# A four-layer graph network in fp32: value rows projected in their own group, next weights spread over six units, stores waited for in the next pass, own bias of the last graph pass on VectorE

## What is computed

```python
# L0, and L3 with other weights and its bias added once: attention with 12 heads of 32 in each graph
q, k, v = heads(x @ Wq.T), heads(x @ Wk.T), heads(x @ Wv.T + bv)
scores  = q @ k.T * 384**-0.5 + adj + adj
p       = softmax(where(any(scores != 0), scores, -inf)), nan_to_num
layer   = (p @ v) @ Wo.T + bo
# L1: q, k, v with biases; adj masks and is added with factor beta; no output matrix
# L2: twice (own weights in each):
attn    = softmax(h @ h.T / sqrt(384)) * adj, rows divided by their sum
ctx     = (attn * upper) @ (h @ Wl.T + bl) + diag(attn) * (h @ Ws.T + bs) + (attn * lower) @ (h @ Wr.T + br)
h       = relu((ctx - mean) / std * gain + shift)
```

## Time and profile before

| | |
|---|---|
| median of three runs | 2626.3 us (2626.18 to 2629.85) |
| the profiled execution | 2625.92 us, of which its span 2624.2 us |
| granted TensorE clock, mean | 0.975 |
| busy: PE / DVE / ACT / POOL | 2445.8 (93%) / 1966.2 (75%) / 1605.0 (61%) / 1966.9 (75%) us |
| passes begin (first matmul after the barrier) | l1 638.1, l20 1176.3, l21 1585.1, l3 2015.4 us |

### The profile page before, as it was taken

The page is one execution under the profiler, slowest core; times in us unless marked ns, Lnnn a source line. Parts: engine busy times, 40 slices in busy tenths (PEclk is TensorE's granted clock), DMA queues, the critical chain, the costliest instruction groups (busy, mean ns, idle before and its releaser), DMA issues. The chain is left out here.

```text
span 2624.2 us, 64888 instructions
## 1 busy us (share of the span) xinstructions
PE 2445.8 (93%) x21554; PEld 2097.4 (80%) x21554; DVE 1966.2 (75%) x3543; ACT 1605.0 (61%) x3414; POOL 1966.9 (75%) x2127
## 2 busy tenths in 40 slices
PE   6999999996999999959999998999997999999997
PEld 5888888885877777748888887888886888888886
DVE  4777788785788888877777776776765677777876
ACT  4667666664666556634544554766665666766665
POOL 4888888884677777765566566999996778888886
PEclk9999999997999999969999998999998999999998
DMA  7222232223433333316323316434343222223211
GB/s 138 67 67 70 69 75 69 59 62 70 85 77 79 79 76 79 80 55 114 72 63 73 70 49 127 102 93 104 90 105 83 51 68 68 70 68 73 61 46 52
DMA packets 320602, 200.71 MB, mean 76 GB/s; under 512 B 243426, under 2 KB 320484, under 8 KB 320484
## 3 DMA queue, kind: packets, MB, share of 16 engines
q1 hardware_dynamic: 317028, 197.93, 32.3%
q10 hardware_dynamic: 3456, 1.28, 0.3%
HBM read 136.22 MB, written 62.91 MB: 76 GB/s over the span
## 5 line engine op out<-in xcount | busy, mean ns | idle before, releaser
L491 PE MATMUL l_ps_p<-xT,w 128*128 128x512 f32 x2304 | 593.7, 404 | 59.1 <-PEq L1588 15.1
L491 PEld LDWEIGHTS l_ps_p<-xT,w 128*128 128x128 f32 x2304 | 425.2, 191 | 154.3 <-issue 39.1
L431 POOL TENSOR_TENSOR l_pr<-l_sc,l_st 128x768 f32<-128x768 f32 x192 | 286.4, 1492 | 176.9 <-DVE l_st L826 176.9
L1353 ACT ACTIVATE l_hlr<-l_ps_h 64x384 f32<-64x384 f32 x512 | 248.8, 486 | 250.1 <-PE l_ps_h L1273 241.4
L836 DVE TENSOR_REDUCE l_st<-l_pr 128x12 f32<-128x768 f32 x192 | 182.8, 952 | 244.3 <-ACT l_pr L703 244.3
L385 POOL TENSOR_TENSOR v<-v,l_bvs 128x768 f32<-128x768 f32 x192 | 359.7, 1873 | 0.0
L1199 POOL TENSOR_TENSOR l_hlr<-l_hlr,l_sides 128x768 f32<-128x768 f32 x128 | 235.8, 1842 | 133.1 <-ACT l_hlr L1353 129.5
L1273 PE MATMUL l_ps_h<-second,xT 128*128 128x384 f32 x1728 | 332.2, 342 | 0.0
L1273 PE MATMUL l_ps_h<-w,xT 128*128 128x384 f32 x1728 | 324.7, 342 | 0.0
L1273 PEld LDWEIGHTS l_ps_h<-second,xT 128*128 128x128 f32 x1728 | 300.1, 189 | 29.8 <-issue 28.7
L1273 PEld LDWEIGHTS l_ps_h<-w,xT 128*128 128x128 f32 x1728 | 299.5, 189 | 29.8 <-issue 27.5
(11 more groups left out here) (144 smaller groups left out, 4577.5 us busy)
## 6 DMA issues: line engine op xcount, KB each, us to landing
rows<-l_yo SPq DMA_DIRECT2D x256, 192.0 KB, 1.9
xa<-rows SPq DMA_DIRECT2D x256, 192.0 KB, 4.2
l_xr<-rows SPq DMA_DIRECT2D x192, 192.0 KB, 2.4
l_xr<-in_x SPq DMA_DIRECT2D x64, 192.0 KB, 2.4
out<-l_yo SPq DMA_DIRECT2D x64, 192.0 KB, 1.9
xa<-in_x SPq DMA_DIRECT2D x62, 192.0 KB, 4.2
l_edge<-in_adj SPq DMA_DIRECT2D x80, 128.0 KB, 2.3
raw<-in_L_gnn_Wk SPq DMA_DIRECT2D x12, 144.0 KB, 6.6
```

What stands on the lines that cost most here:

```text
L431: nc.gpsimd.tensor_tensor(pr[b][:, :, :], sc[b][:, :, :], st[b][:, 0, :].unsqueeze(2).to_broadcast([P, HEADS, NODES]), ALU.subtract).then_ ...
L491: last = nc.tensor.matmul(bank[:, :], W[m][:, l, t, o * P:(o + 1) * P], rows[:, r, t, :], start=c + t == 0, stop=c == 2 and t == KT - 1)
L1353: i = nc.scalar.activation(hlr[b][half * NODES:(half + 1) * NODES, g, :], ps_h[m][g * NODES:(g + 1) * NODES, :D], ACT.Copy)
```

## The change

It has six parts.

1. **Value rows.** `AHEAD` now begins with the four v and `exists`, `made` and `bank_of` are rewritten so that v of group i are made in group i and only q and k in group i−1. Before group 0 stand six projections (`AT_FIRST`), and the last group has four. ScalarE waits and TensorE's waits on its copies are rewritten (`act_first`, `act_k2` for the last k tile). Where unit 3 has nothing in gap 0, ScalarE does gap 1 before exp.
2. **Rows' low parts.** GpSimd makes the last tile of group i+1 in unit 0 and two tiles of group i+2 in units 2 and 3, in place of two and one.
3. **Weights of the next pass.** Two steps in each of the last six units (`steps_at`); turned ones go through two SBUF tiles `wt` in place of the projections' banks.
4. **Stores.** The tiles `yo` and their semaphores are shared by all passes; the wait for a pass's stores moves to SP's stream at the next pass's start.
5. **l21's own bias.** The tenth matmul, its bias row's preparation and ScalarE's copy go; VectorE does `itself` and the diagonal as in l20.
6. **GpSimd's tail** in the graph passes adds residual rows one step earlier.

```diff
@@ attention_pass
+        wt = [a.sb(f"wt{b}", [P, D]) for b in range(2)] if nxt and nxt.turned else None
-        yo = [a.sb(f"yo{b}", [P, D]) for b in range(2)]
+        yo, s_out = shared.yo, shared.s_out
+        out_base = 16 * (units // 2) * me.k
...
-        AHEAD = (("q", 0), ("q", 1), ("q", 2), ("k", 0), ("k", 1), ("k", 2), ("v", 0), ("v", 1), ("v", 2), ("v", 3))
-        BETWEEN = (((), (0,), (1,)), ((), (2,), (3,)), ((4,), (5,), (6,)), ((7,), (8,), (9,)))
+        AHEAD = (("v", 0), ("v", 1), ("v", 2), ("v", 3), ("q", 0), ("q", 1), ("q", 2), ("k", 0), ("k", 1), ("k", 2))
+        BETWEEN = (((0,), (1,), (2,)), ((3,), (), (4,)), ((5,), (6,), (7,)), ((), (8,), (9,)))
+        AT_FIRST = range(4, len(AHEAD))
...
-        def exists(i):
-            return inside(i + 1, groups)
+        def exists(i, pos):
+            return inside(i if AHEAD[pos][0] == "v" else i + 1, groups)
...
+            return tuple(j for j in range(steps) if units - 6 + j // 2 + later == i * UNITS + s)
@@ SP
+            for b in range(2):
+                if out_base:
+                    sp.wait_ge(s_out[b], out_base)
...
-            for b in range(2):
-                sp.wait_ge(s_out[b], 16 * (units // 2))
+            if nxt is None:
+                for b in range(2):
+                    sp.wait_ge(s_out[b], out_base + 16 * (units // 2))
@@ GpSimd, rows_low
-                    for t in ((), (), (0, 1), (2,))[s]:
-                        rows_low(i + 2, par, t)
+                    if s >= 2:
+                        rows_low(i + 2, par, s - 2)
+                    if s == 0:
+                        rows_low(i + 1, 1 - par, 2)
@@ TensorE
-                rows = xT[1 - par]
+                rows = xT[par] if kind == "v" else xT[1 - par]
...
+                    if s == 0:
+                        pe.wait_ge(dve_w, wb + steps)
+                        if isinstance(i, int) and i < 2:
+                            pe.wait_ge(act_first, i + 1)
+                        else:
+                            pe.wait_ge(act_k2[par], pair)
@@ ScalarE
-                    if s < 2:
+                    if not BETWEEN[s][0]:
                         fill(i, par, s, 1)
                         exp(n, s % 2)
...
-                    if nxt and s and isinstance(i, int) and i == groups - 1:
-                        act.wait_ge(pe_p, 10 * groups)
-                        for step in range(KT * (s - 1), KT * s):
-                            weight_high(nxt, step, next_bank(step))
+                    for step in steps_at(i, s, 1):
+                        act.wait_ge(pe_p, dead(step // KT))
+                        weight_high(nxt, step, wt and wt[step % 2])
@@ VectorE
-                        else:
-                            dve.wait_ge(act_v, units)
...
+                    for step in steps_at(i, s, 1):
+                        weight_low(nxt, step, wt and wt[step % 2])
+                    for step in steps_at(i, s, 0):
+                        weight_turned(nxt, step, wt and wt[step % 2], 2)
@@ digcn_pass, SP
-            if ends:
-                for row in (0, 32):
-                    sp.dma_start(brow[row:row + 1, :], row_biases[SELF]).then_inc(s_small, 16)
-            else:
-                sp.dma_start(own[:, :], row_biases[SELF].to_broadcast([P, D])).then_inc(s_small, 16)
+            for b in range(2):
+                sp.wait_ge(s_out[b], out_base)
+            sp.dma_start(own[:, :], row_biases[SELF].to_broadcast([P, D])).then_inc(s_small, 16)
@@ digcn_pass, TensorE
-                if ends and m == SELF:
-                    if isinstance(n, int) and n == 0:
-                        pe.wait_ge(c_row, 3)
-                    last = nc.tensor.matmul(ps_h[m][:, :D], pick[:, :], bias[:, :], start=False, stop=True)
@@ digcn_pass, ScalarE
-                    if ends:
-                        act.wait_ge(pe_h, 3 * n + 3)
-                        act.wait_ge(dve_dg, i + 1)
...
-                        nc.scalar.activation(hs[b][:, :], ps_h[SELF][:, :D], ACT.Copy,
-                                             scale=diag[par][:, s:s + 1]).then_inc(act_h, 1)
@@ digcn_pass, VectorE
-                if ends or not inside(n, units):
+                if not inside(n, units):
                     return
                 dve.wait_ge(pe_h, 3 * n + 3)
                 nc.vector.tensor_tensor(hs[b][:, :], ps_h[SELF][:, :D], own[:, :], ALU.add).then_inc(dve_s, 1)
```

More of the change, by code:

```diff
@@ L93, in __init__ @@
         self.xF = [sb(f"xF{b}", [P, KT, ROWS]) for b in range(2)]
+        self.yo = [sb(f"yo{b}", [P, D]) for b in range(2)]
+        self.s_out = [nc.alloc_semaphore(f"s_out{b}") for b in range(2)]
         self.xT = [sb(f"xT{b}", [P, 2, KT, ROWS], F32R) for b in range(2)]
@@ L256, in attention_pass @@
         s_xr = [a.sem(f"s_xr{b}") for b in range(2)]
-        s_out = [a.sem(f"s_out{b}") for b in range(2)]
         pe_p, pe_s, pe_t, pe_o, pe_y = (a.sem(x) for x in ("pe_p", "pe_s", "pe_t", "pe_o", "pe_y"))
@@ L260, in attention_pass @@
             a.sem(x) for x in ("act_qk", "act_v", "act_e", "act_pT", "act_o"))
+        act_first, act_k2 = a.sem("act_first"), [a.sem(f"act_k2{b}") for b in range(2)]
         dve_off, dve_bias, dve_kb, dve_sc, dve_mx, dve_mn, dve_sum, dve_inv, dve_o = (
@@ L296, in w_bank, with steps_at @@
             return (ps_s, ps_t)[step % 2][:, step % 4 // 2 * 512:step % 4 // 2 * 512 + 512]
-        def next_bank(step):
-            return (*ps_p, ps_y)[step % 3][:, :]
+        def steps_at(i, s, later):
+            if not nxt or not isinstance(i, int):
+                return ()
+            return tuple(j for j in range(steps) if units - 6 + j // 2 + later == i * UNITS + s)
         def has_rows(g):
@@ L415, in _ @@
                     nc.gpsimd.memset(v2[g][:, :, :, :], 0.0).then_inc(shared.c_v2, 1)
-                for t in range(KT):
+                for t in range(KT - g):
                     rows_low(g, g, t)
@@ L444, in _ @@
             over_groups(pool, groups, group)
+            rows_low(groups + 1, 1, 2)
             for n in (units - 2, units - 1):
@@ L680, in _ @@
                 act.wait_ge(dve_kb, 2)
-            for pos in range(len(AHEAD)):
-                if me.k == 0 and pos == 6:
-                    act.wait_ge(shared.c_v2, 2)
+            for pos in AT_FIRST:
                 ahead(-1, 1, pos)
-                if pos in (2, 3, 4):
-                    rows_high(1, 1, pos - 2)
+                if pos in (6, 7, 8):
+                    rows_high(1, 1, pos - 6)
             if wo:
@@ L978, in digcn_pass @@
         loaded = list(shared.loads)
-        own = None if ends else a.sb("own", [P, D])
-        if ends:
-            pick = shared.pick
-            brow = a.sb("brow", [P, D])
-            bround = a.sb("bround", [P, D], F32R)
-            bias = a.sb("bias", [P, D], F32R)
-            c_zero, c_row = a.sem("c_zero"), a.sem("c_row")
+        own = a.sb("own", [P, D])
         sides = a.sb("sides", [P, GPU, D])
@@ L1227, in _ @@
             inner_norm(units - 1, 1)
+            add_rows(units - 2, units // 2 - 1, 0)
             outer_norm(units - 3, 1)
-            for n in (units - 2, units - 1):
-                add_rows(n, units // 2 - 1, n % 2)
-                outer_norm(n, n % 2)
+            add_rows(units - 1, units // 2 - 1, 1)
+            outer_norm(units - 2, 0)
+            outer_norm(units - 1, 1)
         @block.tensor
@@ L1265, in project @@
                     pe.wait_ge(dve_w, wb + KT * (m + 1))
-                if m == SELF and not ends:
+                if m == SELF:
                     if counted(n):
@@ L1536, in outer_stats @@
                 nc.vector.bn_aggr(ln[b][:, 17:19], ln[b][:, 11:17]).then_inc(dve_mv2, 1)
-            if ends:
-                nc.vector.memset(bias[:, :].bitcast(F32), 0.0).then_inc(c_zero, 1)
             dve.wait_ge(c_mask, masks)
```

117 lines of the change are left out of this document (47 added, 70 removed).

## The result

| | before | changed |
|---|---|---|
| median, four runs each | 2626.24 us | 2666.16 us |
| lowest and highest | 2625.4 to 2629.85 | 2663.23 to 2671.39 |
| profiled execution, its span | 2625.92, 2624.2 us | 2663.23, 2661.5 us |
| granted TensorE clock, mean | 0.975 | 0.972 |

The ratio is 1.0153 (95% interval 1.0138 to 1.0168): the change makes the kernel 1.5% slower. I had forecast 2580 with a range up to 2605.

What follows compares the result with a forecast made beforehand. TensorE was taken to bound l0 and l3, with most other gains at the seams. Starts −19.9, stores −6.0, ends −1.7, first groups −0.5, steady groups −3.0 and −2.0, l21 −12.7 summed to −45.8: 2580 us, range 2558 to 2605.

Steps and rivals of the forecast that it cites:

- the steady attention groups: Steady groups of l0, l3 and l1: new projection order about level, −3.0 us for l0 and l3, −2.0 for l1.
- The sign of being wrong: Steady l0 group at 37 us or more with TensorE idle for VectorE behind a late exp, or l21's groups at 25.4.
- (c): l0 and l3: exp waits for the projection in units 3 and 0, 2.6 us per group, +78, 2658; chance 0.06.
- (b): l0 and l3: the chain becomes the bound through later exps, +0.7 us per group, +21, 2604; chance 0.15.
- The starts: Attention passes' starts: v moved behind the first scores, −8.6 us in l0, −4.9 in l1, −6.4 in l3; −19.9 together.
- Stores: Seams between passes: four passes no longer wait for their last stores to land, −6.0 us, range −3.8 to −7.6.
- rival (e): Seams between passes: the barrier waits for the stores' landing anyway, their −6.0 us is nothing, 2586; chance 0.05.
- Ends: Attention passes' ends: spread weight splitting −3.0 us, last groups' four v +0.5 in l1 and +0.8 in l3; −1.7 together.
- rival (f): l1's end: turned weights' low parts from SBUF cost +4.4 us, up to 9.1 more, 2584 to 2594; chance 0.06.
- l21: Pass l21: tenth matmul removed −9.9 us over 15 groups, its start −2.1, its tail −0.7; −12.7 together.
- the tail's 0.7: l21's end: GpSimd adds the last units' residual rows one step sooner, −0.7 us, between 0 and −2.
- I take 2.1 of it: l21's start: TensorE's 2.93 us wait for the bias row goes, −2.1 us counted, between 0 and −2.9.

Runs made afterwards that it cites:

- experiment 2: Changed kernel with ScalarE's exp ahead of gap 1's copies in a group's last unit: 2694.3 us, 1.0256.
- k_early: Changed kernel with the last k one gap earlier in l0 and l3, the last but one also earlier in all three attention passes: 2628.8 us, 1.0012.
- experiment 12: experiment 11's kernel with the next weights split three steps in each of the last three units, turned ones over three SBUF tiles: 2590.55 us, 0.9864.
- experiment 8: Kernel before the change with only l21's own bias moved to VectorE: 2622.3 us, 0.9984.
- experiment 10: Changed kernel, l0 and l3 ordered as in k_early, l1 as in experiment 3, graph passes' second-group edges loaded ahead of the next weights: 2595.8 us, 0.9889.
- experiment 11: experiment 10's kernel with l21's residual rows of units 0 and 1 also loaded ahead of the next pass's weights: 2588.05 us, 0.9855.
- experiment 3: Changed kernel with unit 0's v made last in the group before, only v of units 1 to 3 in their own group, old gap table: 2635.6 us, 1.0037.
- experiment 4: Changed kernel without the value-rows part: all ten projections a group ahead in the old order: 2643.1 us, 1.0072.
- experiment 5: experiment 4's kernel with the rows' high and low parts issued as in the kernel before the change: 2613.6 us, 0.9950.

## Why the prediction was wrong

**The step that failed** is the one on the steady attention groups: "Chain and TensorE stay about level; I take −0.1 per group × 30 groups", and its "−2.0" for l1. Measured: +1.4 per group of l0 and l3, and +2.2 of l1, in all +74 between the first and last scores of the three passes, where −7 was forecast with the ends and first groups. With +1.4 each, the groups of l0 and l3 gave 40 us of it, l1's with +2.2 the rest. The working compared the lengths of what the engines do per unit, and looked for the late instruction inside the units (exp, subtraction). It never asked of each projection's copy how soon its reader comes. The same working had named that very wait at one place, l1's start ("the copy of the last k … becomes TensorE's new wait"): there it is 1.63 us in the changed kernel's trace. With the new order every group ends as that start does. The rows for it were there: a copy of 1.25 us in 30 groups and one of 1.45 in 15 make 59 us at the least, more than the whole sum of 45.8, and would have turned the sign. Measured were 45.6 and 47.4. In l1 the working also had no term for the clock, which took 0.7 to 0.9 us of the 2.2. The sign of being wrong that it named came half: a steady l0 group takes over 37 us, but TensorE is idle for ScalarE's copy of a k and not for VectorE behind a late exp.

**The rivals.** (c) had the direction and nearly the time, 2658, at a chance of 0.06, but by the wrong mechanism, so its number was luck: exp stood behind the copies at no cost in l0 and l3 (experiment 2). Its point of decision, 1.5 us per group, was right for 30 groups; l1's 15 groups were missing from it. (b) is not borne out at its price of 0.7 us per group: k_early's groups are 36.4 and 36.3 us, 0.1 to 0.2 over the kernel before, and whether late exps make that was not separated.

**The starts**: −8.6, −4.9 and −6.4 were forecast. The stretches to l0's, l1's and l3's first scores shrank by 8.6, 9.6 and 9.3, stores included. With 1.9 of stores each, 8.6, 6.8 and 8.3 were forecast: within 3 us, and the surplus of l1 is in line with the earlier end of the weights (experiment 12).

**Stores**: −6.0; alone they gave 4.4 between medians (3.4 to 8.1 by the interval), and 6.6 in the four stretches of the profile. Right, and rival (e) falls.

**Ends**: −3.0 for the spread weights was right within its error (2.5 for l0 and l1 together, in experiment 12, where turned weights still go through SBUF tiles; no run put the old scheme back whole). That turned weights come from SBUF costs less than rival (f) had it. The rows by form in the changed kernel, which answer to the last two of the earlier trace rows:

```profile
L804 DVE TENSOR_TENSOR w<-raw,w 128x384 fp32r<-128x384 f32 x9 | 8.0, 922 | 0.4 <-ACT w L637 0.2
L804 DVE TENSOR_TENSOR w<-l_wt,w 128x384 fp32r<-128x384 f32 x9 | 6.7, 778 | 0.0
```

The low part of a turned matrix takes 778 ns in place of 524, over nine 2.3 us and not 4.4. The Trainium skill's rule (SBUF — State Buffer, Who interferes with whom) says only that two SBUF inputs contend with GpSimd's reads; the trace agrees in sign, and no run here took the tile back to PSUM, so what it costs in the end was not separated.

**l21**: −12.7 was forecast; with 1.1 of stores and without the tail's 0.7, which falls into the next stretch, that is −13.1; the stretch to its first context and l21 itself took 5.8 and 1.5 less, 7.3 together. (By its own factors, 0.65 × 15, the −9.9 in the sum is −9.8.) The steady part was right: most groups take 24.6 to 24.8 us. But the second and the last are 1.4 longer than before, which no term had and no run explains, and the start was wrong. "I take 2.1 of it" counted a wait removed: the first context came sooner by more than that (4.8 in experiment 8), but the next thing waited for was not looked up. GpSimd stood for the edges and the residual rows, loads that do not get earlier when the first matmuls do, and the first group gave back 4.0 us in the changed kernel's profile, 6 to 7 in those of other runs with the same code there. Experiments 10 and 11 show it: with these loads ahead of the weights that group takes 24.7.

## What to carry to other kernels

When an order is changed, take each product, its copy and its first reader, and count what TensorE does between the product's end and that reader: under the copy's length, it is a wait in every turn of the loop. Where TensorE bounds the loop, as in l0, 1.5 us of it cost 1.4; in l1, where TensorE waited anyway, a wait of 1.5 us stood in groups that were 0.2 longer. Put last in a turn what is read latest, and, if experiment 3 is read rightly, share the projections over units so that none falls below the chain. At a pass's start, look in the queue that issues loads for small ones behind large ones that nobody needs yet: moving the edges and two tiles of rows ahead gave 12 us here.

## What the runs showed that I had not expected

- The same wait of 3.04 us ahead of the scores in l1 was followed by a stretch at the lower clock in 11 of 12 steady groups (nine matmuls took 2.97 us in one of them) and by the full clock in one (1.85 us), and between the two kinds lie 0.7 to 0.9 us per group. The clock thus costs less than the wait, but no term of a sum of waits has it. In l0 and l3, with waits of 1.50, the groups' clock stayed at 1.00, and so it did in l1 with waits of 1.5 (experiment 3).
- Moving a k's copy behind exp, an instruction of 0.84 us, lengthened each group of l1 by 2.0 us, the wait itself by 1.3 (experiment 2).
- Two changes that each look like a plain saving (value rows in their own group, and the rows' parts moved) hold each other up: the second without the first costs 2.4 us in each group of l1, the clock's share among them (experiments 4 and 5).
